# Expert groups of three batches and one in place of two and two, and the experts' second matrix read in place

## The chip, the cores and the metric

The kernel runs on one core of one Trainium2 chip. The metric is the time of one execution on the device in microseconds (us). "Before" is the kernel ahead of the change, "after" the changed one.

## What is computed

Four sequences of 512 tokens of width 128 go through six residual layers, all in f32 at the interfaces:

```python
x = x + 0.5 * moe_layer(layernorm(x))          # attention inside, then a routed FFN
x = x + causal_attention(layernorm(x))
x = x + 0.5 * moe_layer(layernorm(x))          # the same weights again
x = x + 0.5 * lora_ffn(layernorm(x))
x = x + causal_attention_2(layernorm(x))
x = x + 0.5 * lora_ffn(layernorm(x))
```

The routed FFN is what the change touches. Each token goes to one of 8 experts, the one with the largest logit:

```python
logits = hn2 @ gate_w + gate_b                 # hn2: (2048, 128)
idx = argmax(logits, axis=-1)
mid = relu(einsum('th,ehf->etf', hn2, w1) + b1[:, None, :])   # f = 512
y   = einsum('etf,efh->eth', mid, w2) + b2[:, None, :]
moe = y[idx, arange(2048)]
```

Attention has 16 heads of 8; the LoRA FFN is dense, 128 to 512 to 128 with two low-rank updates.

## The kernel before

The four sequences pass four attention layers, and the kernel numbers these 16 passes 0 to 15: "batches" 0 to 3 are the first routed layer, 4 to 7 the first causal one, 8 to 11 the second routed layer, 12 to 15 the second causal one. A batch's attention is four "quads" of four heads; a quad is a first pass of scores for the row maxima (`p1` on TensorE, reduced on VectorE), a transposed second pass (`p2`) whose exponentials ScalarE takes, and the product with the values (`pv`). One quad is one unit of the plan's clock.

The plan is one list of events made by `segment()` and `schedule()`. There are three segments: batches 0 to 3, batches 4 to 11, batches 12 to 15. Attention lays down the clock, and everything else is put in by hand-written due times in quads (the tables `PREP`, `NORM_AT`, `ROUTE_AT`, `TILES_AT`, `Y_AT`, `DENSE_AT`, `NEXT_AT`). Each engine's program is the plan's events in that order, so an instruction that waits holds up everything behind it on its own engine.

A routed layer's four batches are taken in groups, `hm` 0 and 1 in the first layer and 2 and 3 in the second. Before, a group is two batches. For each group:

- `lT`, `gate` (TensorE, VectorE): normalised rows transposed and multiplied by the gate matrix, batch by batch.
- `pick`, `rank`, `place0`, `place1`, `place2`: VectorE finds the expert of every token (one-hot `ohb`), TensorE counts ranks within an expert, VectorE makes each token's row number `pos` (place1) and the expert `owner` of each tile of 128 sorted rows (place2). The tokens of an expert are padded up to full tiles, so 8 tiles of tokens may take up to 15.
- `scatter`: GpSimd sends each tile of 128 rows to its sorted place in DRAM with an indirect DMA, one instruction per tile.
- `xload`: SyncE loads the sorted rows back, in two transfers. It waits for all scatters of the group.
- Per tile: `lay` (VectorE copies the owner's weights out of the table `experts`, which holds all eight, into one of NWE buffers `we`, a view of `pt`; the expert's number is first loaded into a VectorE register from `owner`), `tt` (TensorE transposes the rows), hTm (ScalarE copies), `up` (4 matmuls by W1), relu (4 activations, bias b1), `dn` (4 matmuls by W2), the sum with b2 into `ysb` (VectorE), `ysend` (GpSimd sends the rows back to token order in DRAM).
- `yload` (SyncE, waits for all sends of the group), `yadd` (VectorE adds half of it to x).

Since attention uses `pt` for its exponentials and tiles use it for weights, tiles begin after the segment's last `pv`. So the end of segments 1 and 2 is a stretch of tiles with other work put between: at the end of segment 1 the norm, projections and operand "stack" (transfers of `parts` to `qs` and `ks`) of batch 4; at the end of segment 2 the dense LoRA FFN of batches 8 to 11 (`fu0`, `fu1`, `fdn`) and the same for batch 12. The next segment starts with `p1` of batch 4 or 12.

In the profile and the rows, the lines are those of the kernel before: L576 is `p1` and `p2`, L627 `m` (the negated maxima of a quad), L652 `pv`, L660/L665/L670 the output projection, L676 `lT`, L681 `gate`, L687/L690 `rank`, L696 `tt`, L701 `up`, L707 `dn`, L715/L721 the dense FFN, L1049 `lay`, L1057/L1058 the number copy and the sum with b2, L1236 `scatter`, L1241 `ysend`, L1282/L1283 `xload`, L1289 `yload`, L854 the register load of a tile's expert.

Of the kernel before, what the change touches and what calls it, by code (L numbers as in the profile page):

```python
# [13 lines left out]
P = 128  # L14
# [22 lines left out]
TILES = 2 * TB  # L37
SLOTS = TILES + E - 1
ROW = P + 1
NRES = 3  # L40
NWE = 3
NY = 8
FLIPS = TOPK
WE = 2 * F + FB + P
# [34 lines left out]
PREP = [('stats', 7.927), ('rstd', 7.55), ('norm', 7.1), ('hT', 6.9), ('q', 6.7), ('qrem', 6.65), ('k', 6.419),  # L79
        ('krem', 6.553), ('qmid', 6.3), ('kmid', 6.1), ('qlo', 6.05), ('klo', 5.851), ('v', 2.951), ('keep',  # L80
# [21 lines left out]
STACK_FROM, STACK_EVERY = 6.412, 0.253  # L102
# [3 lines left out]
LOADS_FROM, LOADS_EVERY = 2.931, 0.418  # L106
# [1323 lines left out]
```

## Time and profile before

| | |
|---|---|
| time, median of 3 runs | 1017.01 us (1016.29 to 1017.32) |
| profiled execution: its time, its span | 1020.19 us, 1018.4 us |
| mean granted TensorE clock of the profiled execution | 0.966 |
| busy: TensorE, VectorE, ScalarE, GpSimd | 897.5, 779.7, 674.8, 342.2 us |
| chain that ended last: TensorE, VectorE, issue, ScalarE | 53%, 21%, 10%, 10% |

The span is the time from the first to the last instruction of the profiled execution; its 1.8 us to the time lie outside the program's instructions. All places in the program are given below as us from the span's start. A busy time is the union of an engine's instructions. The chain is followed back from the last instruction, at each step to what released it.

### The profile page before, as it was taken

The page shows a single profiled execution, that of the slowest core. Times are in us where ns is not written, and L with a number is a line of the kernel's source. Part 1 is how long each engine was busy: PE and PEld are TensorE (multiplying, and loading weights), DVE is VectorE, ACT ScalarE, POOL GpSimd, SP SyncE. Part 2 cuts the span into 40 slices and gives each one's busy share as a digit, 9 for nine tenths or more (in the row PEclk, how much of TensorE's full clock was granted, in tenths as well). Part 3 has the DMA queues.
Part 4 walks back from the last instruction along what each step waited for, and adds up shares of the span by engine and source line. Part 5 has one row for each costly group of instructions (what it writes and reads, how often), then busy time and mean ns, then how long its engine had stood idle before and what let it go on. Part 6 is the DMA issues. An engine that isn't in the chain of part 4 may idle for free.

```text
span 1018.4 us, 25342 instructions
## 1 busy us (share of the span) xinstructions
PE 897.5 (88%) x10020; PEld 477.1 (47%) x10020; DVE 779.7 (77%) x1412; ACT 674.8 (66%) x1470; POOL 342.2 (34%) x603
## 2 busy tenths in 40 slices
PE   2699999898778799999899999889698989999998
PEld 1123333236767455554323333249685645555465
DVE  5889899855447887888989999817368788888646
ACT  2288887786555577777798878786362358767631
POOL 4444312242646323233232312516571133311100
PEclk8599999999989899999999999999799989999999
DMA  5117740001133221121010200010310222110000
GB/s 146 46 44 178 191 107 2 16 10 47 43 94 85 78 66 35 35 66 43 23 46 22 55 11 2 23 41 30 97 33 24 62 64 65 33 38 4 3 22 21
DMA packets 60520, 52.29 MB, mean 51 GB/s; under 512 B 9106, under 2 KB 57362, under 8 KB 60402
## 3 DMA queue, kind: packets, MB, share of 16 engines
q1 hardware_dynamic: 48980, 40.00, 14.6%
q10 hardware_dynamic: 8478, 4.62, 2.2%
q0 software_dynamic: 2944, 6.05, 1.8%
q8 instruction: 79, 1.29, 0.6%
q14 instruction: 39, 0.32, 0.1%
HBM read 13.64 MB, written 11.06 MB: 24 GB/s over the span
## 4 chain that ended last, share of the span: by engine, by line
PE 53%; DVE 21%; issue 10%; ACT 10%; another core or an unknown queue 2%; DMA 2%; POOL 1%; DVEq 1%; ACTq 0%; SPq 0%; POOLq 0%
PE ps L576 14%; PE ps L652 13%; DVE negm L937 10%; ACT pt L770 7%; PE ps L715 4%; PE ps L607 3%; PE ps L707 3%; PE ps L701 3%; PE ps L582 3%; DVE blockm L928 2%; PE ps L721 2%; PE ps L660 2%; PE ps L612 1%; PE ps L670 1%
## 5 line engine op out<-in xcount | busy, mean ns | idle before, releaser
L770 ACT ACTIVATE pt<-ps 128x512 f32<-128x512 f32 (+1 forms) x896 | 458.3, 567 | 156.1 <-PE ps L576 107.2
L937 DVE TENSOR_REDUCE negm<-ps 128x2 f32<-128x1024 f32 x256 | 300.9, 1219 | 31.0 <-PE ps L576 28.4
L652 PE MATMUL ps<-pt,va 128*32 128x256 f32 (+1 forms) x4352 | 274.3, 341 | 12.1 <-ACT ot L776 5.5
L928 DVE TENSOR_REDUCE blockm<-ps 128x8 f32<-128x1024 f32 (+1 forms) x192 | 195.2, 1042 | 34.2 <-PE ps L576 21.8
L576 PE MATMUL ps<-ks,qs 61*128 61x128 bf16 (+2 forms) x1536 | 174.0, 293 | 35.7 <-DVE negm L937 16.0
L576 PE MATMUL ps<-qs,ks 64*128 64x128 bf16 (+3 forms) x1408 | 168.1, 296 | 7.8 <-ACT pt L770 2.3
L652 PEld LDWEIGHTS ps<-pt,va 128*32 128x32 f32 x4352 | 91.9, 108 | 124.5 <-issue 83.0
L576 PEld LDWEIGHTS ps<-ks,qs 61*128 61x128 bf16 x1536 | 54.8, 95 | 189.8 <-issue 86.6
L1206 POOL CAST mpart<-negm 128x16 bf16<-128x16 f32 x64 | 13.2, 207 | 300.2 <-DVE negm L937 153.8
L804 ACT ACTIVATE stage<-ps,pt 128x128 f32<-128x128 f32 x240 | 68.6, 373 | 41.6 <-PE ps L701 29.8
L1241 POOL DMA_INDIRECT y_rows<-pt,numbers_y x60 | 70.7, 1179 | 63.4 <-DVE pt L1058 55.0
L576 PEld LDWEIGHTS ps<-qs,ks 64*128 64x128 bf16 x1408 | 57.9, 94 | 63.7 <-ACT pt L770 47.0
L701 PE MATMUL ps<-hTm,pt 128*128 128x128 f32 x480 | 68.0, 287 | 15.0 <-DVE pt L1049 12.9
L707 PE MATMUL ps<-pt,stage 128*128 128x128 f32 x480 | 66.5, 283 | 4.5 <-ACT stage L804 3.4
L701 PEld LDWEIGHTS ps<-hTm,pt 128*128 128x128 f32 x480 | 61.4, 200 | 19.0 <-ACT hTm L797 12.0
L1146 POOL TENSOR_TENSOR q<-q,parts 128x512 f32<-128x512 f32 x29 | 33.5, 1156 | 95.0 <-ACT parts L752 94.9
L1049 DVE COPY pt<-experts 128x1156 f32 x60 | 46.7, 785 | 24.0 <-PE ps L652 17.6
L707 PEld LDWEIGHTS ps<-pt,stage 128*128 128x128 f32 x480 | 61.0, 199 | 6.1 <-issue 4.5
L715 PE MATMUL ps<-hTa,wk 128*128 128x512 f32 x128 | 58.6, 599 | 2.3 <-DVE stage L1070 1.6
L810 ACT ACTIVATE stage<-ps 128x512 f32<-128x512 f32 x32 | 19.1, 597 | 37.2 <-PE ps L715 32.4
L797 ACT ACTIVATE hTm<-ps,wpk 128x128 f32<-128x128 f32 x60 | 28.2, 472 | 21.2 <-remote 12.3
L607 PE MATMUL ps<-hT,wpk 128*128 128x512 f32 x64 | 39.0, 699 | 1.7 <-ACT hT L743 0.9
(151 smaller groups left out, 1017.9 us busy)
## 6 DMA issues: line engine op xcount, KB each, us to landing
qs<-parts SPq DMA_DIRECT2D x80, 128.0 KB
ks<-parts SPq DMA_DIRECT2D x77, 128.0 KB
experts<-in_experts SPq DMA_DIRECT2D x8, 578.0 KB, 6.3
sorted<-stage ACTq DMA_DIRECT2D x4, 967.5 KB, 8.3
qs<-mrow SPq DMA_DIRECT2D x128, 6.0 KB
pt<-y_rows SPq DMA_DIRECT2D x8, 256.0 KB, 2.9
qs<-parts SPq DMA_DIRECT2D x32, 56.0 KB
ks<-parts SPq DMA_DIRECT2D x30, 56.0 KB
```

The lines of the kernel that those rows point to most:

```text
L576: ends[s] = pe.matmul(banks[s][:, col:col + c1 - c0], stationary[s][:, i * P:(i + 1) * P], moving[s][:, c0:c1], start=(m_ == 0), stop=(not ...
L607: pe.matmul(b_bank(o), w["w" + name], hT[:, :], start=True, stop=True).then_inc(b_full, 1)
L652: ins = pe.matmul(pv_bank[32 * j:32 * j + 32, q0:q1], va[n % 2][:, kb, value_at(g, j):value_at(g, j) + 32], pt[:, k_, from_:from_ + q1 - q ...
L701: ins = pe.matmul(b_tiles(o)[:, a, :], we[:, number_of(n, at) % NWE, a * P:(a + 1) * P], hTm[:, number_of(n, at) % 2, :], start=True, stop ...
L707: ins = pe.matmul(pair_of(ka)[:, 0, 0:P], mid_e[:, number_of(n, at) % 2, a, :], we[:, number_of(n, at) % NWE, F + a * P:F + (a + 1) * P], ...
L715: pe.matmul(pair_of(ka)[:, 0, :] if kx else b_bank(o), wk[:, kx, at * P:(at + 1) * P], hTa[:, n % 2, :], start=True, stop=True).then_inc(a ...
L770: a.activation(pt[:, k_ % NPT, S * s:S * s + width], b_bank(o + s)[:, 0:width], ACT.Exp).then_inc(b_free, 1)
L804: ins = a.activation(mid_e[:, number_of(n, at) % 2, fb, :], b_tiles(o)[:, fb, :], ACT.Relu, bias=we[:, at_, 2 * F + fb:2 * F + fb + 1])
L928: v.tensor_reduce(blockm[:, g % 2, :, t, PLACES[c_]], pair_of(ka)[:, :, 0:width].rearrange("p s (b c) -> p s b c", c=P), AX, ALU.max, nega ...
L937: v.tensor_reduce(negm[:, g % 2, :, t, c_], pair_of(ka), AX, ALU.max, negate=True).then_inc(a_free, 1)
L1049: v.tensor_copy(we[:, number_of(n, at) % NWE, :], experts[:, bass.ds(next_expert[n], 1), :] .rearrange("p o c -> p (o c)")).then_inc(laid, 1)
L1241: g_.indirect_dma_start(d["y_rows"][n], bass.IndirectOffsetOnAxis(numbers_y[:, r:r + 1], 0), ysb[:, r, :], None).then_inc(y_sent[r], 16)
```

## The change

Groups become three batches and one, `GROUPS = [(0, 1, 2), (3,)] * 2`. A group of three has 12 tiles of tokens and up to 19 tiles, a group of one has 4 and up to 11, so a layer has 30 tiles as before (15 and 15). The first group of a layer can be routed only after the gate of its third batch, which falls in the last quads of the segment's attention; before, it was routed after the gate of the second. The routing's due times in `ROUTE_AT` move accordingly, from 11.1 to 14.4 and from 27.1 to 30.4.

The table `experts` is written in another column order, so that W1, b1 and b2 are neighbours. `lay` copies only these (644 columns in place of 1156), and `dn` takes W2 from `experts` itself, at an expert's number that TensorE loads into a register after each `up`. The sorted rows' numbers are no longer copied to `numbers_y` for `ysend`, which reads them from the rows. There are 4 weight buffers in place of 3, 4 residual buffers in place of 3, 12 buffers for y in place of 8. `xload` of the second layer's first group waits for the sends of the first layer's first group. Due times of tiles, y, the dense FFN and the preparation of batches 4 and 12 are written anew.

```diff
+GROUPS = [(0, 1, 2), (3,)] * 2
+TILES = [TB * len(group) for group in GROUPS]
+SLOTS = [tiles + E - 1 for tiles in TILES]
+MOST, MOST_SLOTS = max(TILES), max(SLOTS)
 ROW = P + 1
-NWE = 3
-NY = 8
+NRES = 4
+NWE = 4
+NY = 12
 FLIPS = TOPK
-WE = 2 * F + FB + P
+WE = F + FB + P
+W2_AT = WE
...
-ROUTE_AT = {0: {'pick': 11.1, 'rank': 11.6, 'place0': 11.8, 'place1': 12.0, 'place2': 12.2, 'scatter': 12.209,
-        'every': 0.15, 'xload': 15.2}, 1: {'pick': 18.304, 'rank': 18.5, 'place0': 19.259, 'place1': 18.75,
-        'place2': 18.95, 'scatter': 18.8, 'every': 0.005, 'xload': 20.0}, 2: {'pick': 27.1, 'rank': 27.6, 'place0':
-        27.8, 'place1': 28.189, 'place2': 28.389, 'scatter': 28.3, 'every': 0.15, 'xload': 31.2}, 3: {'pick': 34.2,
-        'rank': 34.5, 'place0': 34.55, 'place1': 34.598, 'place2': 34.9, 'scatter': 34.362, 'every': 0.005, 'xload':
-        36.0}}
+ROUTE_AT = {0: {'pick': 14.4, 'rank': 14.55, 'place0': 14.7, 'place1': 14.8, 'place2': 14.95, 'scatter': 14.85,
+        'every': 0.1, 'xload': 16.2}, 1: {'pick': 18.304, 'rank': 18.5, 'place0': 18.7, 'place1': 18.75, 'place2':
+        18.95, 'scatter': 18.8, 'every': 0.005, 'xload': 20.0}, 2: {'pick': 30.4, 'rank': 30.55, 'place0': 30.7,
+        'place1': 30.8, 'place2': 30.95, 'scatter': 30.85, 'every': 0.1, 'xload': 32.2}, 3: {'pick': 34.2, 'rank':
+        34.5, 'place0': 34.55, 'place1': 34.58, 'place2': 34.942, 'scatter': 34.876, 'every': 0.261, 'xload':
+        36.256}}
...
-TILES_AT = {0: {'start': 16.75, 'every': 0.207, 'lay0': 0.35, 'lay': 0.384, 'tt': -0.257, 'dn': 0.22699999999999998,
-        'ysend': 0.277}, 1: {'start': 20.401, 'every': 0.207, 'lay0': 0.35, 'lay': 0.384, 'tt': -0.213, 'dn':
+TILES_AT = {0: {'start': 16.75, 'every': 0.207, 'lay0': 0.523, 'lay': 0.48, 'tt': -0.31, 'dn': 0.249, 'ysend':
+        0.299}, 1: {'start': 20.8, 'every': 0.207, 'lay0': 0.35, 'lay': 0.384, 'tt': -0.257, 'dn': 0.227, 'ysend':
...
-DENSE_AT = {8: {'at': 39.75, 'unit': 0.26, 'fdn': 1.05}, 9: {'at': 40.764, 'unit': 0.273, 'fdn': 1.063}, 10: {'at':
-        41.843, 'unit': 0.273, 'fdn': 1.011}, 11: {'at': 44.011, 'unit': 0.221, 'fdn': 1.05}, 12: {'at': 14.2,
+DENSE_AT = {8: {'at': 38.5, 'unit': 0.15, 'fdn': 0.8}, 9: {'at': 39.35, 'unit': 0.15, 'fdn': 0.745}, 10: {'at':
+        40.3, 'unit': 0.15, 'fdn': 0.8}, 11: {'at': 41.2, 'unit': 0.15, 'fdn': 0.8}, 12: {'at': 14.096, 'unit':
...
+        def expert_of(eng, hm, t):
+            k_ = MOST_SLOTS * (hm % 2) + t
+            return eng.value_load(owner[0:1, k_:k_ + 1], min_val=0, max_val=E - 1)
...
+                    need(pe, owner_step, 3 * n + 3)
+                    expert[n, at] = expert_of(pe, n, at)
                 elif name == "dn":
                     need(pe, b_free, at_b[("up", n, at)] + 1)
                     for a in range(FB):
+                        w2 = experts[:, bass.ds(expert[n, at], 1), W2_AT + a * P:W2_AT + (a + 1) * P]
                         ins = pe.matmul(pair_of(ka)[:, 0, 0:P], mid_e[:, number_of(n, at) % 2, a, :],
-                                        we[:, number_of(n, at) % NWE, F + a * P:F + (a + 1) * P], start=(a == 0),
-                                        stop=(a == FB - 1))
+                                        w2.rearrange("p o c -> p (o c)"), start=(a == 0), stop=(a == FB - 1))
                     ins.then_inc(a_full, 1)
...
                     need(v, pv_done, at_pv[final_pv(last_batch(n), 3)] + 1)
                     if tile_before(n, at, NWE):
                         need(v, a_free, at_a[("dn", *tile_before(n, at, NWE))] + 1)
-                    v.tensor_copy(we[:, number_of(n, at) % NWE, :], experts[:, bass.ds(next_expert[n], 1), :]
+                    v.tensor_copy(we[:, number_of(n, at) % NWE, :], experts[:, bass.ds(expert[n, at], 1), 0:WE]
                                   .rearrange("p o c -> p (o c)")).then_inc(laid, 1)
-                    if at + 1 < SLOTS:
-                        next_expert[n] = expert_of(v, n, at + 1)
+                    if at + 1 < SLOTS[n]:
+                        expert[n, at + 1] = expert_of(v, n, at + 1)
                 elif name == "dn":
                     r = number_of(n, at) % NY
                     if tile_before(n, at, NY):
                         need(v, y_sent[r], 16 * (number_of(n, at) // NY))
-                    v.tensor_copy(numbers_y[:, r:r + 1], sorted_rows[n % 2][:, at, P:ROW].bitcast(U32))
                     v.tensor_tensor(ysb[:, r, :], pair_of(ka)[:, 0, 0:P],
-                                    we[:, number_of(n, at) % NWE, 2 * F + FB:WE], ALU.add).then_inc(a_free, 1)
+                                    we[:, number_of(n, at) % NWE, F + FB:WE], ALU.add).then_inc(a_free, 1)
...
                     r = number_of(n, at) % NY
                     g_.wait_ge(a_free, at_a[("dn", n, at)] + 1)
-                    g_.indirect_dma_start(d["y_rows"][n], bass.IndirectOffsetOnAxis(numbers_y[:, r:r + 1], 0),
+                    g_.indirect_dma_start(d["y_rows"][n], bass.IndirectOffsetOnAxis(sorted_rows[n % 2][:, at, P:ROW]
+                                                                                      .bitcast(U32), 0),
                                           ysb[:, r, :], None).then_inc(y_sent[r], 16)
...
                     elif n == 2:
-                        need(sp, a_free, at_a[("dn", 0, SLOTS - 1)] + 1)
+                        for r in range(NY):
+                            need(sp, y_sent[r], 16 * len(range(r, SLOTS[0], NY)))
                     else:
                         need(sp, pv_done, at_pv[final_pv(last_batch(n), 3)] + 1)
-                    for b in (0, 1):
-                        sp.wait_ge(rows_sorted[2 * (n % 2) + b], 16 * TB * (n // 2 + 1))
```

How this moves instructions is seen at three places. In the rows, `[waits ...]` are the semaphores that an instruction waits for, and xN counts equal instructions.

**TensorE, in the last batch's attention of segment 1**, just behind the last `m` (mpart). `pt,va` is `pv`, `qs,ks` is `p2`, `identf,res` is `lT` of batch 2, `identf,ot` the output transposes. Before:

```order
L652 MATMUL ps<-pt,va 32x256 [waits pv_free]
L652 MATMUL ps<-pt,va 32x256 x3
L576 MATMUL ps<-qs,ks 128x512 [waits b_free]
L576 MATMUL ps<-qs,ks 128x512
L676 MATMUL ps<-identf,res 128x128 [waits ln_norm,b_free]
L676 MATMUL ps<-identf,res 128x128 x3
L660 MATMUL ps<-identf,ot 128x128 [waits a_free]
L660 MATMUL ps<-identf,ot 128x128 x3
L652 MATMUL ps<-pt,va 32x256 x4
L576 MATMUL ps<-qs,ks 128x512 [waits b_free]
L576 MATMUL ps<-qs,ks 128x512
```

After, behind the same `m`:

```order
L693 MATMUL ps<-pt,va 32x256 [waits pv_free]
L693 MATMUL ps<-pt,va 32x256 x3
L612 MATMUL ps<-qs,ks 128x512 [waits b_free]
L612 MATMUL ps<-qs,ks 128x512
L722 MATMUL ps<-wpk,hTa 128x8 [waits a_free]
L722 MATMUL ps<-wpk,hTa 128x8 x3
L701 MATMUL ps<-identf,ot 128x128 [waits a_free]
L701 MATMUL ps<-identf,ot 128x128 x3
L693 MATMUL ps<-pt,va 32x256 x4
L612 MATMUL ps<-qs,ks 128x512 [waits b_free]
L612 MATMUL ps<-qs,ks 128x512
L729 MATMUL ps<-ohb,earlier 128x96 [waits const_done,picked,a_free]
```

The gate of batch 2 (`wpk,hTa`) stands now where its `lT` stood, four `p2` pairs earlier, and the ranks of group 0 (`ohb,earlier`), which stood about three quads ahead, follow it with a wait for `picked`. Segment 2 has the same order at its end.

**TensorE, two tiles in a row.** `identf,...` is `tt`, `hTm,pt` is `up`. Before, `dn` is `pt,stage`:

```order
L696 MATMUL ps<-identf,stage 128x128
L701 MATMUL ps<-hTm,pt 128x128 [waits laid,b_free]
L701 MATMUL ps<-hTm,pt 128x128 x3
L707 MATMUL ps<-pt,stage 128x128 [waits b_free,a_free]
L707 MATMUL ps<-pt,stage 128x128 x3
L696 MATMUL ps<-identf,stage 128x128
```

After, `dn` is `experts,pt`, and `owner` is the tile's expert:

```order
L738 MATMUL ps<-identf,pt 128x128
L743 MATMUL ps<-hTm,pt 128x128 [waits laid,b_free]
L743 MATMUL ps<-hTm,pt 128x128 x3
L625 TENSOR_LOAD owner
L625 ISA x2
L752 ISA [waits b_free,a_free]
L752 MATMUL ps<-experts,pt 128x128
L752 ISA
L752 MATMUL ps<-experts,pt 128x128
L752 ISA
```

Behind every `up` stand now a register load and two register operations, and an address operation ahead of each of the four matmuls of `dn`; the first of these carries the waits of `dn`. There are 60 tiles in the program.

**GpSimd, from the last scatters of group 0 to those of group 1.** `sorted<-res,pos` is a scatter, `y_rows` a send, the rest are norms and residuals. Before:

```order
L1221 TENSOR_TENSOR res<-res,upd 128x4x128 [waits h_kept,a_free]
L1241 DMA y_rows<-pt,numbers_y 2944x128 [waits a_free] x2
L1227 TENSOR_SCALAR l_tmp<-l_mv 128x4 [waits ln_rstd,ln_stat]
L1229 TENSOR_TENSOR l_rstd<-l_tmp,minus_half 128x4 [waits ln_rstd]
L1241 DMA y_rows<-pt,numbers_y 2944x128 [waits a_free] x7
L1236 DMA sorted<-res,pos 1920x129 [waits ln_norm,placed]
L1236 DMA sorted<-res,pos 1920x129 [waits placed] x3
L1236 DMA sorted<-res,pos 1920x129 [waits ln_norm,placed]
L1236 DMA sorted<-res,pos 1920x129 [waits placed] x3
L1241 DMA y_rows<-pt,numbers_y 2944x128 [waits a_free] x7
```

After:

```order
L1282 DMA sorted<-res,pos 2432x129 [waits prefilled,placed]
L1282 DMA sorted<-res,pos 2432x129 [waits placed] x3
L1282 DMA sorted<-res,pos 2432x129 [waits ln_norm,placed]
L1282 DMA sorted<-res,pos 2432x129 [waits placed] x3
L1282 DMA sorted<-res,pos 2432x129 [waits ln_norm,placed]
L1282 DMA sorted<-res,pos 2432x129 [waits placed] x3
L1267 TENSOR_TENSOR res<-res,upd 128x4x128 [waits h_kept,a_free]
L1287 DMA y_rows<-pt,stage 3968x128 [waits a_free]
L1273 TENSOR_SCALAR l_tmp<-l_mv 128x4 [waits ln_rstd,ln_stat]
L1275 TENSOR_TENSOR l_rstd<-l_tmp,minus_half 128x4 [waits ln_rstd]
L1287 DMA y_rows<-pt,stage 3968x128 [waits a_free] x8
L1282 DMA sorted<-res,pos 1408x129 [waits ln_norm,placed]
```

Group 1's eight scatters stood between the first nine sends of group 0 and its last six. Now the twelve scatters of group 0 stand in one run, all behind the attention's last `mpart`, and group 1 has four (the last row is the first of them), between nine sends of group 0 and its last ten.

## Rows read from the trace of the kernel before

**Rows 1.** The page, busy time by engine: us, share of the span, instructions.
```profile
PE 897.5 (88%) x10020; PEld 477.1 (47%) x10020; DVE 779.7 (77%) x1412; ACT 674.8 (66%) x1470; POOL 342.2 (34%) x603
```

**Rows 2.** Stretches: length, busy PE, PEld, DVE, ACT, POOL; granted clock, DMA share, GB/s.
```profile
238.58:275.00 36.42, 32.04 (x281) 30.38 (x277) 23.24 (x75) 23.50 (x74) 20.53 (x19) 1.00 0.09 27
275.00:290.00 15.00, 7.53 (x37) 6.70 (x38) 3.12 (x9) 3.44 (x12) 7.69 (x8) 0.66 0.37 109
290.00:325.85 35.85, 30.93 (x252) 28.48 (x250) 22.30 (x72) 23.94 (x75) 23.69 (x20) 1.00 0.29 82
680.09:716.00 35.91, 33.10 (x288) 31.35 (x284) 23.77 (x77) 23.45 (x74) 19.61 (x18) 1.00 0.08 26
716.00:730.20 14.20, 5.49 (x28) 5.07 (x28) 2.75 (x7) 3.43 (x11) 9.00 (x9) 0.75 0.39 111
730.20:811.95 81.75, 76.97 (x463) 58.21 (x462) 57.64 (x159) 36.22 (x95) 28.73 (x29) 0.98 0.16 46
```

**Rows 3.** TensorE in order of time, first segment's end and two tiles.
```profile
220.06 0.66 PE L676 MATMUL ps<-identf,res 128*128 128x128 f32 x4
...
238.58 0.33 PE L696 MATMUL ps<-identf,stage 128*128 128x128 f32 x1
...
264.00 1.06 PE L701 MATMUL ps<-hTm,pt 128*128 128x128 f32 x8
...
265.90 1.06 PE L701 MATMUL ps<-hTm,pt 128*128 128x128 f32 x8
```

**Rows 4.** TensorE in order of time, second segment's end.
```profile
663.30 0.65 PE L676 MATMUL ps<-identf,res 128*128 128x128 f32 x4
...
680.09 0.33 PE L696 MATMUL ps<-identf,stage 128*128 128x128 f32 x1
...
699.42 0.96 PE L681 MATMUL ps<-wpk,hTa 128*128 128x8 f32 x8
...
721.71 0.47 PE L696 MATMUL ps<-identf,pt 128*128 128x128 f32 x1 [5.67 <-DMA pt<-sorted]
```

**Rows 5.** GpSimd in order of time: a y row sent, scatters of the second group.
```profile
285.73 1.22 POOL L1241 DMA_INDIRECT y_rows<-pt,numbers_y  x1 [1.92 <-DVE pt L1058]
...
706.31 1.26 POOL L1236 DMA_INDIRECT sorted<-res,pos  x1 [5.10 <-DVE pos L1030]
...
715.99 0.96 POOL L1236 DMA_INDIRECT sorted<-res,pos  x1 [0.30 <-issue]
```

**Rows 6.** SyncE's queue: first and last of the 18 transfers of batch 4's stack.
```profile
302.52 1.90 SPq L1312 DMA_DIRECT2D qs<-parts  x3
...
315.23 0.59 SPq L1312 DMA_DIRECT2D ks<-parts  x1
```

**Rows 7.** VectorE's register loads (ns, min/median/max), all 60.
```profile
L854 DVEq TENSOR_LOAD <-owner x60: 298/304/548, 194.5 to 755.7; - x60
L854 DVEq FUSED_REGOPS  x60: 183/190/206, 195.1 to 756.0; - x60
```

**Rows 8.** VectorE in order of time: three lays in one run.
```profile
285.37 2.15 DVE L1049 COPY pt<-experts 128x1156 f32 x3
```

**Rows 9.** The page, costliest groups: the lay (busy us, mean ns).
```profile
L1049 DVE COPY pt<-experts 128x1156 f32 x60 | 46.7, 785 | 24.0 <-PE ps L652 17.6
```

**Rows 10.** TensorE's waits, 238 to 326 and 680 to 812: us, times, longest.
```profile
PE ps L701 <- DVE pt L1049: 7.5, 5, 4.2
...
PE ps L687 <- DVE ohb L1006: 0.7, 1, 0.7
...
PE ps L701 <- DVE pt L1049: 5.4, 4, 3.0
```

**Rows 11.** Busy us of three quads of attention, columns as in rows 2.
```profile
190.57:205.04 14.47, 11.57 (x97) 4.01 (x101) 11.61 (x19) 8.89 (x18) 5.97 (x10) 0.88 0.08 25
205.04:217.21 12.17, 11.66 (x122) 3.34 (x125) 11.74 (x19) 9.97 (x20) 6.25 (x10) 1.00 0.06 19
635.15:647.55 12.40, 10.20 (x97) 3.98 (x101) 11.41 (x19) 8.76 (x18) 4.83 (x8) 1.00 0.07 24
```

More of the change, by code:

```diff
@@ L146, in tiles_of @@
 def tiles_of(hm):
-    T, jobs = TILES_AT[hm], []
-    for t in range(SLOTS):
+    T, jobs, lay = TILES_AT[hm], [], -NEVER
+    for t in range(SLOTS[hm]):
         up = T["start"] + T["every"] * t
-        jobs += [(up - (T["lay0"] if t < 2 else T["lay"]), "lay", hm, t), (up + T["tt"], "tt", hm, t),
+        lay = max(lay, up - (T["lay0"] if t < 2 else T["lay"]))
+        jobs += [(lay, "lay", hm, t), (up + T["tt"], "tt", hm, t),
                  (up, "up", hm, t), (up + T["dn"], "dn", hm, t), (up + T["ysend"], "ysend", hm, t)]
@@ L159, in routing, with batch_of, group_of @@
             (("pick", None), ("rank", None), ("place", 0), ("place", 1), ("place", 2), ("xload", None))] + \
[L160 removed]
+        [(R["scatter"] + R["every"] * j, "scatter", hm, j) for j in range(TILES[hm])]
+def batch_of(hm, k):
+    return NB * (hm // 2) + GROUPS[hm][k]
+def group_of(l):
+    hm = 2 * (l // NB) + (l % NB not in GROUPS[0])
+    return hm, GROUPS[hm].index(l % NB)
 def returns(hm):
[L164 removed]
+    return [(Y_AT[hm]["yload"], "yload", batch_of(hm, k), None) for k in range(len(GROUPS[hm]))]
 def sums(hm):
[L168 removed]
+    Y = Y_AT[hm]
+    return [(max(Y[f"yadd{j}"] for j in range(k + 1)), "yadd", batch_of(hm, k), None) for k in range(len(GROUPS[hm]))]
 def norms(l):
@@ L247, in segment, with in_order @@
     return out
+ROUTING = [("pick", None), ("rank", None), ("place", 0), ("place", 1), ("place", 2)]
+COUNTED = ("lay", "tt", "up", "dn", "xfold", "yadd", "lstats", "lrstd", "lnorm", "stats", "rstd", "norm", "keep", "out")
+def in_order(plan):
+    at = {ev: i for i, ev in enumerate(plan) if ev[0] in ("gate", "pick", "rank", "place")}
+    steps = [ev for hm in range(4) for ev in [("gate", batch_of(hm, k), None) for k in range(len(GROUPS[hm]))] +
+             [(name, hm, k) for name, k in ROUTING]]
+    assert all(at[a] < at[b] for a, b in zip(steps, steps[1:]))
+    for name in COUNTED:
+        counted = [ev[1:] for ev in plan if ev[0] == name]
+        assert counted == sorted(counted, key=lambda ev: (ev[0], ev[1] or 0)), (name, counted)
+    return plan
 def schedule(causal_of):
@@ L553, in number_of @@
         def number_of(hm, t):
-            return hm * SLOTS + t
+            return sum(SLOTS[:hm]) + t
         def tile_before(hm, t, back):
-            return divmod(number_of(hm, t) - back, SLOTS) if number_of(hm, t) >= back else None
+            if number_of(hm, t) < back:
+                return None
+            return (hm, t - back) if t >= back else tile_before(hm - 1, SLOTS[hm - 1] - 1, back - t - 1)
         def last_batch(hm):
@@ L1016, in dve_program @@
-                    step(v.tensor_reduce(ntile[:, :], more[:, :, :], AX, ALU.add))
+                    step(v.scalar_tensor_tensor(more[:, :, 0:nt], ranks[:, nt:nt + 1, :].rearrange("p o e -> p e o")
+                                                .broadcast_to([P, E, nt]), 1.0 / P,
+                                                count[:, 0:nt].rearrange("p (o k) -> p o k", o=1)
+                                                .broadcast_to([P, E, nt]), ALU.mult, ALU.is_gt))
+                    step(v.tensor_reduce(ntile[:, :], more[:, :, 0:nt], AX, ALU.add))
@@ L1230, in pool_program @@
                 elif name == "scatter":
[L1231 removed]
+                    i = batch_of(n, at // TB)
                     g_.wait_ge(placed, n + 1)
```

246 lines of the change are left out of this document (123 added, 123 removed).

## The prediction

> **What bounds the kernel now.** I read the page's busy times first, then the stretches where a segment of attention has ended and tiles run, then TensorE, GpSimd and SyncE in order of time there, and last TensorE's waits. TensorE is busy 897.5 of 1018.4 us [rows 1]: about 120 us are not its work, and only from these can a change of order take time, since the matmuls stay the same 60 tiles. In the tile stages TensorE is the bound while tiles flow: one follows the other in 265.90 - 264.00 = 1.90 us [rows 3]. But each stage has a hole between its two groups. In 275 to 290 TensorE is busy 7.53 of 15.00, in 716 to 730.2 it is 5.49 of 14.20, and the granted clock is 0.66 and 0.75, a mixture of its two levels (1.2 and 2.4 GHz) [rows 2]. The reader sees why in segment 2: the second group's gate starts at 699.42, its scatters run from 706.31 to 716.95, and the first `tt` comes at 721.71 after 5.67 us of idle TensorE [rows 4, 5]. The first group of a stage has no such hole: its `tt` follows the attention at once (238.58, 680.09) [rows 3, 4], because it was routed quads earlier.
>
> **Part 1: the middle hole goes.** The second group is now four scatters, between nine sends and ten sends of a first group of 19 tiles. The four that remain cost 4 x 1.26 us (0.96 and a gap of 0.30 [rows 5]) and have ten tiles of 1.90 us behind which to land. I take both holes as gone: idle 15.00 - 7.53 = 7.47 and 14.20 - 5.49 = 8.71 us [rows 2].
>
> **Part 2: a hole opens at the front.** The first group now waits for its third batch's gate. Gate to first `tt` took 721.71 - 699.42 = 22.29 us with 8 scatters [rows 4]. Twelve add 4 x 1.26 = 5.04, so 27.3. Of the 6.89 us from gate to first scatter [rows 4, 5] I take 0.9 off, since the tiles between which that ranking stood are not there yet; so 26.4, with 24.9 and 28.0 as ends. After, the gate stands in the place of `lT`, at 220.06 and 663.30 [rows 3, 4]. So the first `tt` comes at 246.5 and 689.7 in place of 238.58 and 680.09: +7.9 and +9.6. Behind `tt` on TensorE stand batch 3's output transposes, so nothing else fills this time. The clock will fall here as it did in the middle; that price moves along and I count it at nothing.
>
> Set against each other: segment 1 had 87.27 us from its first `tt` to the next segment's `p1` (238.58 to 325.85), 70.50 busy and 16.77 idle, of which 7.47 in the hole [rows 2]. After: 246.5 + 70.5 + 9.3 = 326.3, or +0.4. Segment 2: 131.86 us, 115.56 busy, 16.30 idle; 689.7 + 115.56 + 7.59 = 812.9, or +0.9. Moving the hole alone gains nothing.
>
> **Part 3: the lay.** TensorE waited for lays 7.5 us in stage 1 and 5.4 in stage 2, of which 4.2 and 3.0 in the holes [rows 10]: 3.3 + 2.4 = 5.7 us lie among flowing tiles. The copy falls from 1156 to 644 columns. Its price before is 785 ns [rows 9]; by columns it would be 437, and a fixed part raises that, so I take 0.5 (ends 0.44 and 0.79). One buffer more and no number copy help too. I take two thirds of 5.7: -3.8 (ends 0 and -5.7).
>
> **Part 4: routing leaves the attention's quads.** The quad in which the first group's last placing stood took 14.47 us at a clock of 0.88, the next 12.17 [rows 11]; its twin in segment 2 took 12.40, no more than usual. I take -2.3 and 0 (ends 0 and -4.6 together). In the tail the ranks wait for `picked`; that wait cost 0.7 in a like place [rows 10], so twice +0.7. Net -0.9.
>
> **Part 5: TensorE's register loads.** Behind each `up` TensorE's own sequencer loads a register and takes two operations. On VectorE a load took 304 ns and its operation 190 [rows 7]: 0.49 us, 60 times is 29.6 us if nothing covers it. VectorE shows that it can be covered: three lays with their loads between took 2.15 us, 0.72 each, less than a lay's mean [rows 8, 9]; the loads cost nothing there. On TensorE the cover is the `up` just issued, 4 matmuls of 1.06 us together [rows 3]. I take nothing, with 29.6 as the far end. For such a load the Trainium skill ("DMA: Bandwidth & Descriptors", Latency and other measured facts) gives a floor of about 600 ns; by it the uncovered price would be an estimated 36 us, and the row's 304 ns disagrees with it. The same skill ("TensorE: Matmul & The Clock Gate", the paragraph on NX overlap) says that the sequencer takes up the next instruction once one is committed, by which the load would be covered; no run here shows that for TensorE.
>
> **What is late next in segment 1.** The first group's last tile ends later. From a last send (285.73) to the end of batch 4's stack (315.23 + 0.59 = 315.82) went 30.1 us [rows 5, 6]. After, 19 tiles of 1.90 from 246.5 end near 290.6 with about 8 of the 13.5 us that the stage's 70.5 busy us hold beside 30 tiles; the send comes near 291.5, the stack near 321.6. `p1` is due at 326.3 less part 3's 2.2, so 2.5 us are left. No price, but little room.
>
> **The sum.** +0.4 + 0.9 - 3.8 - 0.9 = -3.4 us, made against the profiled 1020.19 us; the median of the runs shown is 1017.01, so 1013.6, and I say 1013.
>
> **Rivals.**
> 1. More comes off: the gate reaches its `tt` in 24.9 us, all lay waits go, the quads give 4.6. That is -3.0 - 1.9 - 2.3 below my sum, 1006. For it: the routing runs in a tail where VectorE has few reductions left. Against: the twin quad of segment 2 showed no price to win back. Chance 0.21.
> 2. The front hole is longer than the middle one, and the stack becomes the limit: 28.0 us from gate to `tt` gives 1.6 each, and every us by which the stack lands after 324.1 counts in full. With 3 us of that: 1013.6 + 3.2 + 3 = about 1020, slower. It decides from 5.4 us on top of my sum. For it: twelve scatters stand alone in front of everything. Against: they go in the emptiest queue. Chance 0.16.
> 3. The register loads are not covered. In full 1013.6 + 29.6 = 1043; it decides when 0.09 us of each of the 60 shows on TensorE (5.4 / 60). For it: `dn` waits for relu with its address operations still to come, so the sequencer can lose its lead. Against: rows 8. Chance 0.10.
> 4. The middle hole stays, since group 1's scatters wait behind GpSimd's sends, and the change does not do what it is written for: 1013.6 + 7.5 + 8.7 = 1030. Against: ten tiles stand behind them. Chance 0.03.
>
> **How the numbers follow.** My forecast, between -1 and -7, has 0.50. About 0.2% (2 us) is what a measurement of this kernel can tell from no change. The forecast is faster in 0.36 and the same in 0.14; the first rival is faster; the second is the same in 0.04 and slower in 0.12; the third and fourth are slower. Faster 0.57, same 0.18, slower 0.25. The range leaves out most of the third and fourth rivals and the far end of the first: 1001 to 1025; the forecast's own is 1010 to 1016.
>
> **What would show it.** In the profile after: idle TensorE of 7 to 11 us ahead of the first `tt` of each stage, released by the rows' transfer; no such idle between the groups; lays of about 0.5 us and waits for them under 2 us in all; the quad after 190 near 12.2 us; a tile still every 1.90 us. A tile of 2.0 or more proves the loads' cost; a wait of `p1` of batch 4 for `ks` or `qs` proves the stack. I am wrong if the tail hides the twelve scatters, or if matmuls with addresses from a register go slower by themselves.

## The result and the profile after

The changed kernel takes 1006.40 us (median of 3 runs, 1004.1 to 1008.38); the ratio to the kernel before is 0.9896, interval 0.9861 to 0.9931. Five more runs of it beside the experiments gave 1004.75 us and 0.9892 (0.9874 to 0.9909): about 11 us faster, where 4 were forecast. The profiled execution after has a span of 1004.6 us, that before 1018.4, so the two profiles differ by 13.8; the profiled execution of before lay 3.2 us above its median.

The page after: busy us by engine, the `up` matmuls with the idle time ahead of them, and the lay (answers to [rows 1, 9]):

```profile
PE 892.1 (89%) x10020; PEld 475.5 (47%) x10020; DVE 760.4 (76%) x1352; ACT 674.7 (67%) x1470; POOL 332.2 (33%) x603
...
L743 PE MATMUL ps<-hTm,pt 128*128 128x128 f32 x480 | 65.8, 282 | 0.9 <-ACT pt L848 0.9
...
L1098 DVE COPY pt<-experts 128x644 f32 x60 | 31.1, 519 | 22.8 <-PE ps L693 19.7
```

TensorE in order of time at the end of segment 1 (answers to [rows 3]): the gate of batch 2, the ranks, the last `pv`, the first `tt`, `up` and `dn`, and `p1` of batch 4. The line numbers are those of the kernel after.

```profile
215.05 1.06 PE L722 MATMUL ps<-wpk,hTa 128*128 128x8 f32 x8
...
217.89 0.20 PE L729 MATMUL ps<-ohb,earlier 128*128 128x96 bf16 x1 [0.40 <-issue]
...
232.99 1.07 PE L693 MATMUL ps<-pt,va 128*32 128x256 f32 x16 [0.60 <-ACT pt L814]
241.15 0.47 PE L738 MATMUL ps<-identf,stage 128*128 128x128 f32 x1 [7.09 <-DMA stage<-sorted]
...
242.48 1.86 PE L743 MATMUL ps<-hTm,pt 128*128 128x128 f32 x8
...
246.57 1.06 PE L752 MATMUL ps<-experts,pt 128*128 x8
```

```profile
317.81 0.61 PE L612 MATMUL ps<-ks,qs 61*128 61x128 bf16 x8 [4.38 <-DMA ks<-parts]
```

The same for segment 2 (answers to [rows 4]); 647.98 is `lT` of batch 6, 722.92 the first `tt` of the second group.

```profile
647.98 0.63 PE L717 MATMUL ps<-identf,res 128*128 128x128 f32 x4 [2.68 <-DVE res L1029]
...
653.53 1.06 PE L722 MATMUL ps<-wpk,hTa 128*128 128x8 f32 x8
...
669.78 1.07 PE L693 MATMUL ps<-pt,va 128*32 128x256 f32 x16 [0.60 <-ACT pt L814]
679.36 0.47 PE L738 MATMUL ps<-identf,stage 128*128 128x128 f32 x1 [8.51 <-DMA stage<-sorted]
```

```profile
722.92 0.33 PE L738 MATMUL ps<-identf,pt 128*128 128x128 f32 x1 [1.72 <-DMA pt<-sorted]
```

GpSimd in order of time, the first and the last of the twelve scatters (answers to [rows 5]):

```profile
221.23 1.24 POOL L1282 DMA_INDIRECT sorted<-res,pos  x1 [5.88 <-DVE pos L1077]
...
235.43 0.98 POOL L1282 DMA_INDIRECT sorted<-res,pos  x1 [0.30 <-issue]
```

The reader sees the hole at the front, 7.1 and 8.5 us of idle TensorE, both released by the transfer of the sorted rows, and its cause: twelve scatters from 221.23 to 236.41, in a row that ends 3.4 us after the last `pv` began, and 4.7 us more until the rows are back and the first `tt` starts. The middle hole is gone in segment 1, and 1.72 us of it are left in segment 2. The account of the whole, from the two profiles:

| stretch | before, us | after, us | change |
|---|---|---|---|
| start to the quad with `pick` (its GpSimd cast at 178.74 and 177.04) | 178.7 | 177.0 | -1.7 |
| the two quads that held the routing of segment 1 | 26.3 | 20.9 | -5.4 |
| from there to the last `pv` | 32.5 | 35.1 | +2.5 |
| last `pv` to first `tt` | 1.0 | 8.2 | +7.2 |
| first `tt` to `p1` of batch 4 | 87.3 | 76.7 | -10.6 |
| `p1` of batch 4 to the last `pv` of segment 2 | 353.2 | 352.0 | -1.3 |
| last `pv` to first `tt` | 1.0 | 9.6 | +8.6 |
| first `tt` to `p1` of batch 12 | 131.9 | 120.0 | -11.9 |
| segment 3 | 206.5 | 205.2 | -1.2 |

The quads need a closer look, since they are where I saw little to win. Stretches of the kernel before, columns as in [rows 2]: the two quads ahead of those of [rows 11].

```profile
178.74:190.57 11.83, 10.44 (x116) 3.21 (x116) 11.20 (x19) 9.75 (x20) 0.83 (x5) 1.00 0.01 3
...
623.33:635.15 11.82, 10.44 (x116) 3.19 (x116) 11.19 (x19) 9.74 (x19) 0.83 (x5) 1.00 0.00 1
```

And after, the same quads:

```profile
177.04:186.76 9.72, 9.47 (x97) 2.76 (x97) 9.51 (x9) 8.83 (x18) 0.83 (x4) 1.00 0.02 4
186.76:197.91 11.15, 10.69 (x105) 4.20 (x109) 10.02 (x11) 9.68 (x20) 0.83 (x4) 1.00 0.02 3
613.91:623.63 9.72, 9.47 (x97) 2.76 (x97) 9.51 (x9) 8.83 (x17) 0.84 (x5) 1.00 0.01 3
623.63:634.78 11.15, 10.69 (x105) 4.21 (x109) 10.02 (x11) 9.68 (x20) 0.83 (x5) 1.00 0.01 3
```

Without routing a pair of these quads takes 9.72 + 11.15 = 20.87 us in both segments. Before it took 11.83 + 14.47 and 11.82 + 12.40: the routing cost 5.4 and 3.4 us. VectorE, which had 11.2 to 11.6 us of work in each, has 9.5 and 10.0.

TensorE's waits from 238 to 320, the three longest (answers to [rows 10]):

```profile
PE ps L738 <- DMA stage<-sorted: 7.1, 1, 7.1
PE ps L612 <- DMA ks<-parts: 4.4, 1, 4.4
PE ps L642 <- DVE lnx L937: 2.3, 2, 1.6
```

No wait for a lay is left here, nor in the whole program (the page's row of `up`: 0.9 us idle ahead of it, all from ScalarE). The second row is new: `p1` of batch 4 waits for its stack.

Last the two tile stages after, from the first `tt` to the next segment's `p1`, in three stretches each (answers to [rows 2], the same columns):

```profile
241.15:280.00 38.85, 38.16 (x330) 37.88 (x331) 21.05 (x69) 28.18 (x91) 22.12 (x22) 0.96 0.24 70
280.00:297.00 17.00, 15.20 (x132) 14.59 (x130) 8.30 (x27) 12.48 (x43) 9.55 (x11) 1.00 0.26 79
297.00:317.81 20.81, 14.17 (x104) 12.03 (x104) 9.78 (x32) 10.68 (x29) 11.76 (x12) 0.95 0.38 104
679.36:720.00 40.64, 40.16 (x339) 39.54 (x340) 20.60 (x72) 28.93 (x93) 22.17 (x23) 0.94 0.19 54
720.00:730.00 10.00, 7.83 (x67) 7.38 (x67) 3.01 (x9) 6.11 (x21) 4.46 (x5) 1.00 0.46 137
730.00:799.36 69.36, 65.42 (x371) 46.37 (x370) 49.12 (x132) 27.69 (x67) 21.20 (x24) 0.98 0.15 42
```

TensorE is busy 67.53 and 113.41 us in them, where it was 70.50 and 115.56 for the same matmuls. As a mean over each of these stretches the granted clock is 0.94 to 1.00, where the stretches with the middle holes had 0.66 and 0.75; it still falls at the front, to 0.56 from 242.40 to 244.40 us, behind the hole of segment 1.

### The profile page after: what moved, and what is told of

Its sections match the earlier page's. It is cut to its first block, busy times and chain, and to the rows that moved or that the text cites. A ratio compares the mean times of both kernels' runs of the same rounds, so it can differ in the third digit from the quotient of the medians.

```text
span 1004.6 us, 25715 instructions
## 1 busy us (share of the span) xinstructions
PE 892.1 (89%) x10020; PEld 475.5 (47%) x10020; DVE 760.4 (76%) x1352; ACT 674.7 (67%) x1470; POOL 332.2 (33%) x603
## 4 chain that ended last, share of the span: by engine, by line
PE 57%; DVE 17%; ACT 10%; issue 9%; POOL 4%; DMA 3%; SPq 1%; ACTq 1%; DVEq 0%; POOLq 0%
PE ps L612 14%; PE ps L693 13%; DVE negm L977 8%; ACT pt L814 7%; PE ps L743 5%; PE ps L752 4%; PE ps L759 4%; PE ps L648 3%; DVE blockm L968 3%; PE ps L618 3%; PE ps L765 3%; POOL sorted L1282 2%; PE ps L701 2%; PE ps L653 1%; PE ps L711 1%
## 5 line engine op out<-in xcount | busy, mean ns | idle before, releaser
L977 DVE TENSOR_REDUCE negm<-ps 128x2 f32<-128x1024 f32 x256 | 301.0, 1219 | 26.7 <-PE ps L612 25.7
L848 ACT ACTIVATE pt<-ps,pt 128x128 f32<-128x128 f32 x240 | 68.8, 372 | 26.3 <-PE ps L743 26.2
L743 PE MATMUL ps<-hTm,pt 128*128 128x128 f32 x480 | 65.8, 282 | 0.9 <-ACT pt L848 0.9
L752 PE MATMUL ps<-experts,pt 128*128 x480 | 64.1, 276 | 2.2 <-ACT pt L848 1.3
L752 PEld LDWEIGHTS ps<-experts,pt 128*128 128x128 f32 x480 | 58.5, 192 | 4.2 <-issue 4.1
L1106 DVE TENSOR_TENSOR pt<-ps,pt 128x128 f32<-128x128 f32 x60 | 17.4, 290 | 49.5 <-PE ps L752 48.5
L1098 DVE COPY pt<-experts 128x644 f32 x60 | 31.1, 519 | 22.8 <-PE ps L693 19.7
L1287 POOL DMA_INDIRECT y_rows<-pt,stage x38 | 37.8, 994 | 19.0 <-DVE pt L1106 11.0
L648 PE MATMUL ps<-hT,wpk 128*128 128x512 f32 x64 | 41.4, 736 | 2.2 <-ACT hT L787 1.8
## 6 DMA issues: line engine op xcount, KB each, us to landing
sorted<-stage ACTq DMA_DIRECT2D x2, 1225.5 KB, 11.1
```

Of the source, the lines that this page charges most:

```text
L648: pe.matmul(b_bank(o), w["w" + name], hT[:, :], start=True, stop=True).then_inc(b_full, 1)
L743: ins = pe.matmul(b_tiles(o)[:, a, :], we[:, number_of(n, at) % NWE, a * P:(a + 1) * P], hTm[:, number_of(n, at) % 2, :], start=True, stop ...
L752: ins = pe.matmul(pair_of(ka)[:, 0, 0:P], mid_e[:, number_of(n, at) % 2, a, :], w2.rearrange("p o c -> p (o c)"), start=(a == 0), stop=(a ...
L848: ins = a.activation(mid_e[:, number_of(n, at) % 2, fb, :], b_tiles(o)[:, fb, :], ACT.Relu, bias=we[:, at_, F + fb:F + fb + 1])
L977: v.tensor_reduce(negm[:, g % 2, :, t, c_], pair_of(ka), AX, ALU.max, negate=True).then_inc(a_free, 1)
L1287: g_.indirect_dma_start(d["y_rows"][n], bass.IndirectOffsetOnAxis(sorted_rows[n % 2][:, at, P:ROW] .bitcast(U32), 0), ysb[:, r, :], None). ...
```

## The experiments

My theory after reading the two profiles: the regrouping moves the hole to the front at nearly the same price and takes the routing out of the attention's quads; the narrow lay takes the waits for lays away; the register loads on TensorE are covered. Rivals: the narrow lay does all; the regrouping does all; the loads cost something.

**1. The regrouping alone.** W2 is laid again and read from the buffer; the due times are those of after, but for later lays.

```diff
-NWE = 4
-NY = 12
+NWE = 3
+NY = 5
...
-WE = F + FB + P
-W2_AT = WE
+WE = F + FB + P + F
+W2_AT = F + FB + P
...
-                    expert[n, at] = expert_of(pe, n, at)
...
-                        w2 = experts[:, bass.ds(expert[n, at], 1), W2_AT + a * P:W2_AT + (a + 1) * P]
+                        w2 = we[:, number_of(n, at) % NWE, W2_AT + a * P:W2_AT + (a + 1) * P]
```

> The changed kernel with the whole of an expert laid again (1156 columns, three weight buffers, five y buffers so that they fit, lays due a little later) and no register loads on TensorE; groups, routing and all other due times as after. My theory: the regrouping moves the hole and takes the routing out of the attention's quads, worth about 5 us, and the narrow lay is worth about 5 more by itself; then this run stands at 1010 to 1013. Rival (the narrow lay and the loads do all of it, the regrouping nothing): 1016 to 1018. Second rival (regrouping does all): 1005 to 1008.

Measured: 1010.37 us, ratio 0.9950 (0.9935 to 0.9965). Its waits for lays, and the lay:

```profile
PE ps L743 <- DVE pt L1096: 2.5, 4, 1.2
```

```profile
L1096 DVE COPY pt<-experts 128x1156 f32 x60 | 47.1, 787 | 27.0 <-PE ps L693 19.7
```

Both rivals fall: the regrouping, with the due times that came with it, is worth 5 us of the 11. With groups of 19 and 11 even the wide lay makes TensorE wait only 2.5 us, against 12.9 before, since 7.2 of these lay in the middle holes.

**2. The narrow lay and W2 in place alone**, on the kernel before.

```diff
-WE = 2 * F + FB + P
+WE = F + FB + P
+W2_AT = WE
...
+                    expert[n, at] = expert_of(pe, n, at)
...
+                        w2 = experts[:, bass.ds(expert[n, at], 1), W2_AT + a * P:W2_AT + (a + 1) * P]
...
-                                        we[:, number_of(n, at) % NWE, F + a * P:F + (a + 1) * P], start=(a == 0),
-                                        stop=(a == FB - 1))
+                                        w2.rearrange("p o c -> p (o c)"), start=(a == 0), stop=(a == FB - 1))
```

> The kernel before with W2 read in place and the narrow lay alone; groups of two and two, three weight buffers, the copies of the numbers, all due times as before. My theory: TensorE's waits for lays fall from 12.9 us to some 5 (the two in the middle holes stay, released by the gate), the hole stays, so 1012 to 1014. Rival (the narrow lay does all): 1005 to 1008. Rival of the register loads (they show on TensorE): over 1018.

Measured: 1014.10 us, ratio 0.9976 (0.9965 to 0.9987). TensorE's waits for the rows and for lays:

```profile
PE ps L702 <- DMA pt<-sorted: 10.0, 2, 5.7
...
PE ps L707 <- DVE pt L1057: 5.1, 3, 2.9
```

The hole stays, as the theory has it. The waits for lays fall from 12.9 to 5.1 us, but the wait for the rows grows from 5.7 to 10.0, since the 4.2 us that TensorE spent on a lay in the hole of segment 1 it now spends on the rows; 2.4 us come off the time. Together the two halves give 0.50 + 0.24 = 0.74% of the 1.08% measured for the whole; the rest, 3 to 4 us (1 to 6 by the intervals), belongs to what neither run has (four weight buffers and twelve for y along with the regrouping) or to their sum being more than the parts, and I did not take it further apart.

**3. Every register load on TensorE twice.**

```diff
+                    expert_of(pe, n, at)
                     expert[n, at] = expert_of(pe, n, at)
```

> The changed kernel with every register load on TensorE done twice, 60 more loads of about 0.30 us and their operations of 0.15. If they are covered by the matmuls issued ahead of them: 1005 to 1008, as after. If TensorE's sequencer is at its limit, up to 60 x 0.47 = 28 us more: 1010 to 1034.

Measured: 1013.63 us, ratio 0.9976 (0.9964 to 0.9988), 8 to 9 us above after: within the second range, near its low end, so part of the second load is covered. First the loads of after (ns, min/median/max), and two of its tiles in order of time:

```profile
L625 PEldq TENSOR_LOAD <-owner x60: 296/302/502, 242.2 to 742.8; - x60
L625 PEldq FUSED_REGOPS  x60: 151/151/165, 242.7 to 743.2; - x60
L625 PEldq SEQ_ASSERT  x60: 18/18/28, 243.0 to 743.4; - x60
```

```profile
250.36 1.06 PE L743 MATMUL ps<-hTm,pt 128*128 128x128 f32 x8
251.25 1.06 PE L752 MATMUL ps<-experts,pt 128*128 x8
...
252.26 1.06 PE L743 MATMUL ps<-hTm,pt 128*128 128x128 f32 x8
```

And the run with twice as many:

```profile
267.52 1.06 PE L743 MATMUL ps<-hTm,pt 128*128 128x128 f32 x8
268.48 1.19 PE L753 MATMUL ps<-experts,pt 128*128 x8
...
269.62 1.06 PE L743 MATMUL ps<-hTm,pt 128*128 128x128 f32 x8
```

After, tiles follow each other in 252.26 - 250.36 = 1.90 us as before [rows 3], so one load of 0.30 + 0.15 + 0.02 = 0.47 us is covered. With two, a tile takes 269.62 - 267.52 = 2.10 us, and the delay sits ahead of `dn`, which starts 0.96 after `up` in place of 0.89, and ahead of what follows. So the cover ends between 0.47 and 0.94 us per tile: of 28 us, 8 to 9 show. The Trainium skill's floor of about 600 ns for such a load ("DMA: Bandwidth & Descriptors", Latency and other measured facts) is not what these rows show: 302 ns on TensorE, 304 on VectorE.

**4. The routing late, groups as before.**

```diff
-NRES = 3
+NRES = 4
...
-ROUTE_AT = {0: {'pick': 11.1, 'rank': 11.6, 'place0': 11.8, 'place1': 12.0, 'place2': 12.2, 'scatter': 12.209,
+ROUTE_AT = {0: {'pick': 14.4, 'rank': 14.55, 'place0': 14.7, 'place1': 14.8, 'place2': 14.95, 'scatter': 14.85,
```

(and the same for the first group of segment 2). In this kernel the placing of group 0 writes over the gate's logits of the next batch, with which it shares scratch, so those tokens go to other experts; tiles and instructions are as before.

> The kernel before with four residual buffers and the first group of each layer routed at the due times of after, in the last quads, still groups of two and two. It separates the price of the routing within the quads from the regrouping. My theory: the quad after 190 falls from 14.5 to about 12 us and the next one gains too, 4 to 5 us in segment 1 and 1 to 2 in segment 2; with 8 scatters the first transposes come 3 us (segment 1) and 5 us (segment 2) after the last pv, 2 and 4.5 later than before; the middle holes stay: together 1015 to 1019. Rival (the quads' price was not the routing): quads as before and 1021 to 1024.

Measured: 1015.72 us, ratio 1.0001 (0.9989 to 1.0013). The quads of its profile, columns as in [rows 2]:

```profile
177.98:187.70 9.72, 9.47 (x97) 2.76 (x97) 9.51 (x9) 8.83 (x18) 0.83 (x4) 1.00 0.01 4
187.70:198.85 11.15, 10.69 (x105) 4.20 (x109) 10.02 (x11) 9.68 (x20) 0.83 (x4) 1.00 0.02 3
620.00:629.72 9.72, 9.47 (x97) 2.76 (x97) 9.51 (x9) 8.83 (x18) 0.83 (x4) 1.00 0.01 1
629.72:640.87 11.15, 10.69 (x105) 4.20 (x109) 10.01 (x11) 9.68 (x20) 0.84 (x5) 1.00 0.01 3
```

The same 9.72 and 11.15 as after, to the hundredth: the routing was the price, and the rival falls. The first `tt` of either group in both segments:

```profile
235.16 0.33 PE L696 MATMUL ps<-identf,stage 128*128 128x128 f32 x1 [2.56 <-DMA stage<-sorted]
...
279.08 0.69 PE L696 MATMUL ps<-identf,pt 128*128 128x128 f32 x2 [5.61 <-DMA pt<-sorted]
...
677.06 0.48 PE L696 MATMUL ps<-identf,stage 128*128 128x128 f32 x1 [4.18 <-DMA stage<-sorted]
...
719.30 0.47 PE L696 MATMUL ps<-identf,pt 128*128 128x128 f32 x1 [6.33 <-DMA pt<-sorted]
```

Of the 8.8 us that the quads give, the new holes at the front take 6.9 (2.6 and 4.3 us longer from the last `pv` to the first `tt`), the middle holes stay, and by the medians nothing is left. So late routing alone is worth nothing; in after, the regrouping closes the middle holes beside it.

**5. Work put into the front hole.** The last batch's output projection stands ahead of the first `tt` on TensorE.

```diff
+    if hm % 2 == 0:
+        at = 16 + 8 * hm
+        jobs = [(at + 1.01 + 0.05 * (j[0] - at), *j[1:]) if j[1] != "lay" and j[0] < at + 1.12 else j for j in jobs]
```

> The changed kernel with the last batch's output projection (8 transposes and 4 matmul calls of batch 3, and of batch 11 in segment 2) put ahead of the first tile's transposes on TensorE, so that it runs in the front hole instead of behind it. If the front hole is on the path and TensorE is the bound behind it, as I hold: about 2.7 us of matmuls and 0.7 of a wait come off in each of two stages, so 5 to 7 below after. Rival (the transfers of the stack and of y set the end of the stages, not TensorE): within 2 of after.

> The changed kernel itself, for a narrower interval beside the other runs: 1004 to 1008.

Measured: 1002.62 us, ratio 0.9859 (0.9839 to 0.9879); after, beside it, 1004.75 and 0.9892 (0.9874 to 0.9909). So some 2 to 3 us, half of what I expected and between it and the rival, with intervals that just touch. TensorE's wait for the sorted rows, two of them, falls from 15.6 us in all (8.5 the longest) to

```profile
PE ps L615 <- DMA ks<-parts: 7.5, 2, 4.3
...
PE ps L741 <- DMA stage<-sorted: 4.4, 2, 2.7
```

and first `tt` to `p1` of the next segment from 76.7 to 74.8 and from 120.0 to 116.3 us. Segment 1 gives less than it should, as `p1` still waits 4.3 us for `ks`.

**6. Two of batch 4's stack pieces from ScalarE's queue.**

```diff
+NEXT_ON_ACT = [(1, 1), (0, 5)]
...
-                    if n == 0 and at in ON_ACT:
+                    if n == 0 and at in ON_ACT or n == 4 and at in NEXT_ON_ACT:
...
```

> The changed kernel with two of the twelve stack pieces of batch 4 issued from ScalarE's queue. In the profile after, p1 of batch 4 waits 4.4 us for ks from parts, behind 18 transfers on SyncE's queue that take 14 us. If that queue is what it waits for: 2 to 3 us of the wait go, 2 to 3 below after. Rival (the wait ends with the casts of the parts, not with the queue): as after.

Measured: 1003.23 us, ratio 0.9871 (0.9853 to 0.9889), below after by 1.5 us, with intervals that overlap. In its profile `p1` of batch 4 comes at 314.89 us in place of 317.81, and in TensorE's waits from 280 to 318 the 4.4 us for `ks` have become

```profile
PE ps L613 <- DMA qs<-parts: 1.7, 1, 1.7
```

So the queue was what it waited for, and 2.7 us of the wait go; of the time 1.5 us by the medians, which is not clear of the noise.

**7. Experiments 5 and 6 together.**

> Both of the former edits. If they add: 7 to 10 below after, 997 to 1000. If the queue's wait only swallows what TensorE gives in stage 1: 4 to 6 below after.

Measured: 1000.52 us, ratio 0.9847 (0.9833 to 0.9860), 4 to 5 us below after: about the sum of the two as measured, less than I had expected of them. It also lies in the range of the second case, so it does not tell whether the two add.

**8. The norm of batch 6 earlier.** After, TensorE waits 2.68 us for it (the row at 647.98 above): its due time was left at 29.9 while the `lT` behind it went to 30.0, and six reductions got in between.

```diff
         'lnorm': 25.9, 'lT': 26.4, 'gate': 26.8}, 6: {'lstats': 29.05, 'lrstd': 29.05, 'xfold': 29.25, 'lnorm':
-        29.9, 'lT': 30.0, 'gate': 30.4}, 7: {'lstats': 33.25, 'lrstd': 33.25, 'xfold': 33.35, 'lnorm': 33.65, 'lT':
+        29.5, 'lT': 30.0, 'gate': 30.4}, 7: {'lstats': 33.25, 'lrstd': 33.25, 'xfold': 33.35, 'lnorm': 33.65, 'lT':
```

> The changed kernel with one due time moved: the norm of batch 6 (lnorm 29.9 to 29.5 quads), as far ahead as its neighbours were moved. In the profile after, TensorE waits 2.7 us for it at the transposes of batch 6, behind six reductions on VectorE, and batch 2's has no such wait. If that wait is on the path of the last gate: 2 to 3 us below after, and the front hole of segment 2 keeps its length from gate to first transposes. Rival (the reductions that the norm then holds up cost as much): within 1 of after.

Measured: 1003.07 us, ratio 0.9879 (0.9863 to 0.9894). The `lT` of that profile, with no wait ahead of it:

```profile
644.16 0.66 PE L717 MATMUL ps<-identf,res 128*128 128x128 f32 x4
```

`p1` of batch 4 to the last gate falls from 335.7 to 332.8 us, all of the 2.7; but of the time only some 1.5 us show, within the intervals. Gate to first `tt` is 25.7 us (after: 25.8), so the front hole moved along.

**9. All three.**

> The output projection in the front holes, two stack pieces on ScalarE's queue and the earlier norm of batch 6 together. If the three add: 4 us from the first two as measured together and 2 to 3 more, so 997 to 999. If the norm's gain is swallowed: 1000 to 1001.

Measured: 998.96 us, ratio 0.9829 (0.9815 to 0.9842), at the upper end of what adding would give. That beats both kernels, by 17 us and by 6.

## Why the prediction went as it did

**Direction right, size too small.** The mechanisms of the sum were there, but several of its terms were mis-sized, nearly all the same way. By the profiles I had -3.4 us and 13.8 came off. Of the 10.4 us between, 4.2 lie in the two tile stages with the holes ahead of them (parts 1 to 3), 1.9 in the end of the attention (part 4), and 4.3 in stretches that the forecast did not name:

- **Part 1, the middle hole goes.** It did, except 1.7 us in segment 2 (the row at 722.92).
- **Part 2, the front hole.** Forecast +7.9 and +9.6, measured +7.2 and +8.6. Gate to first `tt` took 26.1 and 25.8 us against 26.4: the mechanism and its price held. That the hole is on the path fits experiment 5 against after and 7 against 6: filling it took 2 to 3 us off each time, but with intervals that touch or overlap. Of the clock I had written "that price moves along and I count it at nothing". In segment 1 the price fell: TensorE's busy time in the tile stage was 70.5, 72.7 and 72.6 us in the profiles with the middle hole (before, experiments 2 and 4) and 67.5 to 68.9 in five with the hole at the front (after, its repetition, experiments 1, 6 and 8), for the same matmuls at a higher clock. That is 1.6 to 5.1 us, which come with the regrouping. In segment 2 the two sets overlap, 112.8 to 115.6 and 111.9 to 113.5, so the 2.1 us between the two profiles above show nothing.
- **Part 3, the lay.** Forecast -3.8. I took two thirds of the 5.7 us outside the holes; after has no such wait at all. In segment 1 the stage's idle time fell from 16.77 to 9.13 us, 4.4 of it the stack's new wait; I had 7.1 left. Experiments 1 and 2, with 2.5 and 5.1 us of such waits, show that neither the regrouping nor the narrow lay takes them all away alone.
- **Part 4, the routing in the quads. This step failed in its reading**: "I take -2.3 and 0", because "its twin in segment 2 took 12.40, no more than usual". The quads that I took as usual carried work of their own. Only the same quad without the routing is the measure: 20.87 us for the pair, in after and in experiment 4 alike, so the price was 5.4 and 3.4. Most of it was given back between there and the last `pv`: +2.5 in segment 1 (32.5 to 35.1) and +3.5 in segment 2 (31.5 to 35.0), where I had +0.7 each. In experiment 4, whose norms kept their places, these stretches took 32.7 and 30.9 us. So what cost it is something that the changed kernel alone has there, the earlier norms and gates or the routing of 12 tiles; 2.7 of segment 2's are the wait of experiment 8, and the rest was not taken apart. The net, -2.9 and +0.1, was near my -1.6 and +0.7, but for two errors that cancel.
- **Part 5, the loads.** Covered, as said; experiment 3 shows both that and how little room was left. The reason given, that the sequencer runs ahead of the array, is the one that the Trainium skill gives in "TensorE: Matmul & The Clock Gate" (the paragraph on NX overlap); the tile of 1.90 us agrees with it for one load.
- **What is late next.** I saw the stack coming 2.5 us ahead of `p1`; it came last, and `p1` waited 4.4 us for it. The last piece was issued by 315.91 (below), 5.7 us ahead of my 321.6, but TensorE was done at 313.4, where I had 324.1. So the stack of the second rival is in the program after, though not its longer hole nor its sum. In experiment 6 2.7 us of this wait go, and 1.5 us of the time, within the noise.

```profile
315.32 0.59 SPq L1362 DMA_DIRECT2D ks<-parts  x1
```

- **The first rival** had 1006, and 1006.4 was measured. That is luck in part: no wait for lays is left, as it says, but the gate did not reach its `tt` in 24.9 us, and the quads gave 8.8 us in place of 4.6, of which 6.0 went again ahead of the last `pv`. The rest of what came off stands in none of its terms.

**Not forecast at all:** -1.7 us ahead of any routing, -1.2 in segment 3, -1.4 from `p1` of batch 4 to the two quads of segment 2. The change also moves due times in the preparation of the first batches (`PREP`, `SECOND`, `STACK_EVERY`, `LOADS_FROM`), which the section on it does not list. GpSimd's cast in the quad that begins at 142.62 us before stands at 142.91 and 141.87 in experiments 2 and 4, which have the due times of before, and between 140.25 and 141.46 in the nine profiles that have those of after: by the means 1.4 us come with what was changed ahead of that place. That the re-timing is the cause is not shown, since no run moves it alone; but the 5 us of experiment 1 hold about 1 us of this (its cast stands at 141.39). The others were not taken apart; segment 3 differs by as much between two profiles of one kernel (205.2 and 206.8 us).

## What to carry to other kernels

Here regrouping moved the hole between two groups and did not close it; what paid is in part what the move set free, work that left a stretch in which its engine was the bound (VectorE is busy 9.51 of 9.72 us in the quad without it). The price of a piece of work in a pipelined stretch is read against the same stretch without it; where no trace has that, what its engine's busy time holds of it was a lower bound here (3.3 and 3.1 us of VectorE per pair of quads, against prices of 5.4 and 3.4), and a neighbour with other work in it is no measure. And after each gain the next wait is worth a look: a free engine ahead of a wait takes work that stands behind it, and a long row of transfers can be split over a second queue.

## What the runs showed of the hardware

A register load and its two operations on TensorE took 302 + 151 + 18 ns, and one of them per tile of 1.90 us cost nothing, while a second one cost 0.15 us per tile over the 60 (some 9 us). After 7.1 us without work the first `up` took 1.86 us in place of 1.06 for the same 8 matmuls, with a granted clock of 0.56 from 242.40 to 244.40, near the lower of its two levels; `dn` at 246.57, 4 us later, took 1.06 again, at 1.00 from there to 250.00 (the rows at the end of segment 1).
